# Expert up products of a Mamba and MoE layer: weights stationary, turned rows moving

## The reference, cut to what matters

```python
def _moe(x, gate_w, w1, w2, w3):
    xf = x.reshape(-1, H)
    logits = xf @ gate_w.T
    rw, sel = jax.lax.top_k(logits, TOP_K)
    rw = jax.nn.softmax(rw, axis=-1)
    out = jnp.zeros_like(xf)
    for e in range(E):
        we = jnp.sum(jnp.where(sel == e, rw, 0.0), axis=-1)
        h = jax.nn.silu(xf @ w1[e].T) * (xf @ w3[e].T)      # up products
        out = out + h @ w2[e].T * we[:, None]               # down product
    return out.reshape(B, S, H)
```

## Time and profile before

| | |
|---|---|
| median of 3 runs | 3352.16 us (3351.89 to 3358.85) |
| profiled execution | 3366.11 us |
| its span, first to last instruction | 3364.7 us |
| PE busy over the span | 86% |
| DVE, ACT, POOL busy | 72%, 57%, 32% |
| expert loop | 2844.0 to 3273.5 us |
| steady part of it (2870 to 3262 us) | PE busy 392.00 of 392.00 us |
| gather and sum behind it | 3273.5 to 3364.7 us |

### The profile page before, as it was taken

How to read it: one execution, slowest core, us unless ns; L and a number is a source line. 1 busy time by engine, 2 the same in 40 slices (tenths; PEclk the granted TensorE clock), 3 DMA queues, 4 the chain that set the end, 5 groups by cost and what they waited for, 6 DMA issues and landing times. The chain is left out here.

```text
span 3364.7 us, 45342 instructions
## 1 busy us (share of the span) xinstructions
PE 2891.2 (86%) x12880; PEld 1110.5 (33%) x12881; DVE 2419.1 (72%) x2674; ACT 1913.4 (57%) x3514; POOL 1090.7 (32%) x652
## 2 busy tenths in 40 slices
PE   5798889899765849999999999999999772999990
PEld 1234334334332512222222222222222252666650
DVE  0699999999997758888888888888888173111113
ACT  3556655665642417788787878787887611222220
POOL 2889778778862530000000000000000045000006
PEclk8999999999998969999999999999999975999995
DMA  1111111111111532111111111111110145111114
GB/s 42 42 50 48 41 55 56 38 51 49 40 44 43 180 96 39 39 39 39 39 39 39 39 34 37 37 39 39 39 39 10 43 148 188 44 47 44 46 36 147
DMA packets 123093, 185.25 MB, mean 55 GB/s; under 512 B 30224, under 2 KB 77968, under 8 KB 122896
## 3 DMA queue, kind: packets, MB, share of 16 engines
q1 hardware_dynamic: 109072, 142.95, 15.0%
q0 software_dynamic: 13824, 39.86, 3.7%
HBM read 138.01 MB, written 44.43 MB: 54 GB/s over the span
## 5 line engine op out<-in xcount | busy, mean ns | idle before, releaser
L1529 DVE TENSOR_REDUCE nmh<-ring 128x2 f32<-128x1024 f32 x1024 | 1195.9, 1219 | 198.3 <-PE ring L1406 198.1
L1387 ACT ACTIVATE prob<-s_ps 128x512 f32<-128x512 f32 x2048 | 1073.0, 603 | 284.2 <-PE s_ps L1427 284.2
L767 DVE TENSOR_TENSOR_SCAN h<-dA,state,bx 128x512 f32<-128x512 f32 x512 | 618.0, 1263 | 117.3 <-ACT dA L606 117.3
L391 POOL TENSOR_TENSOR bx<-u,bb 128x2048 f32<-128x2048 f32 x128 | 578.8, 4527 | 193.7 <-DVE h L767 193.5
L1427 PE MATMUL s_ps<-qs,ks 98*128 98x512 bf16 x2048 | 614.8, 388 | 17.9 <-issue 12.2
L1439 PE MATMUL acc<-prob,vst 128*32 128x512 f32 x4096 | 550.0, 609 | 0.2 <-ACT prob L1387 0.2
L606 ACT ACTIVATE dA<-dt,aneg 128x512 f32<-128x512 f32 x512 | 348.8, 691 | 270.4 <-DVE h L767 270.3
L673 PE MATMUL y_ps<-h,ident 128*128 128x512 f32 x1024 | 480.4, 613 | 1.1 <-DVE h L774 1.1
L1406 PE MATMUL ring<-k,q 64*128 64x512 bf16 x2048 | 348.6, 395 | 43.6 <-DMA k<-parts 23.9
L1427 PEld LDWEIGHTS s_ps<-qs,ks 98*128 98x128 bf16 x2048 | 149.4, 97 | 582.4 <-ACT prob L1387 474.9
L774 DVE TENSOR_TENSOR h<-h,c_ps 128x2048 f32<-128x2048 f32 x128 | 289.6, 2262 | 4.5 <-PE c_ps L652 4.2
(11 more groups left out here) (221 smaller groups left out, 2562.9 us busy)
## 6 DMA issues: line engine op xcount, KB each, us to landing
bb<-b_rows SPq DMA_DIRECT2D x128, 256.0 KB, 3.2
q<-parts SPq DMA_DIRECT2D x256, 64.0 KB, 2.1
parts<-part POOLq DMA_DIRECT2D x48, 256.0 KB, 3.1
qs<-parts SPq DMA_DIRECT2D x192, 64.0 KB, 2.7
ks<-parts SPq DMA_DIRECT2D x192, 64.0 KB, 2.8
xt<-slots_in POOLq DMA_DIRECT2D x72, 128.0 KB, 2.3
slots_out<-yt SPq DMA_DIRECT2D x72, 128.0 KB, 1.7
k<-parts SPq DMA_DIRECT2D x256, 32.0 KB, 2.0
```

The source lines that it names most:

```text
L391: nc.gpsimd.tensor_tensor(bx[:, n % BR], u[:, b], bb[:, n % RB, None, :].to_broadcast([P, KI, CH]), ALU.mult).then_inc(s_bx, 1)
L767: nc.vector.tensor_tensor_scan(h[:, n % HR, d, :], dA[:, d % 2, :], bx[:, n % BR, d, :], state[:, b, n, d:d + 1], ALU.mult, ALU.add).then_ ...
L1387: nc.scalar.activation(prob[:, k % PR, j, :], s_ps[:, tile % SR, :], ACT.Exp, scale=SC).then_inc(s_exp, 1)
L1529: nc.vector.tensor_reduce(nmh[:, slot, t, 2 * s:2 * s + 2], ring[:, s, :, :], AX.X, ALU.max, negate=True).then_inc(s_free[s], 1)
```

## The change

The up products change sides. The stationary operand is now a 128x128 piece of the expert's weights, and the moving operand is `xT`, 128 columns (rows of x). The product then has the inner features in the partitions, which is the form the down product needs, so that the four transposes of `mid` and ACT's copy of them go. The 4 matmuls of 512 columns become 16 matmuls of 128 columns.

A piece of weights as stationary operand is read from a fixed place: for each tile DVE copies the expert's `w1` and ACT its `w3` (128 partitions x 1024 floats each) into `wu`, two slots. Both engines read the expert's number into a register for that (`weights_of`). DVE's product now writes `midT` directly. PE's order in a step becomes: rows of j+1 turned, up products of j, down product of j-1. PE reads the expert's number once a tile, just ahead of the down product, not twice. `wu` takes the room of `g`, which moves to the scope of part (2); since that memory is used again in part (3), POOL now waits for its scatters at the end of part (2), ahead of the common wait of all engines, and not only at the start of part (3).

```diff
@@ part (2), end of POOL's program
+                pool.wait_ge(s_sc, 16 * (2 * NT + NE))
...
+            wu = sb3("wu", [P, 2, 2, KM, FI])
-            m_ps = ps3("m_ps", [P, KF, P])
...
+            def weights_of(eng, w, j):
+                e = eng.value_load(expert[0:1, bass.ds(j, 1)], min_val=0, max_val=NE - 1)
+                return w[:, bass.ds(e, 1), :, :].rearrange("p o k n -> p (o k n)")
@@ ACT
+                def gather_w3(j, q):
+                    src = weights_of(act, w3, j)
+                    wait(act, s_up, j - 1)
+                    nc.scalar.copy(wu[:, q % 2, 1].rearrange("p k n -> p (k n)"), src).then_inc(s_wu3, 1)
...
-                    if there(j, 1):
-                        wait(act, s_mp, j)
-                        wait(act, s_dn, j - 2)
-                        nc.scalar.copy(midT[:, (q - 1) % 2], m_ps[:, :, :]).then_inc(s_mT, 1)
+                        gather_w3(j + 1, (q + 1) % 4)
@@ DVE
+                def gather_w1(j, q):
+                    src = weights_of(dve, w1, j)
+                    wait(dve, s_up, j - 1)
+                    nc.vector.tensor_copy(wu[:, q % 2, 0].rearrange("p k n -> p (k n)"), src).then_inc(s_wu1, 1)
...
-                        wait(dve, s_mp, j - 1)
-                        nc.vector.tensor_tensor(mid[:, q % 2, :], sl[:, q % 2, :], c_ps[:, q % 2, :], ALU.mult
+                        wait(dve, s_dn, j - 1)
+                        nc.vector.tensor_tensor(midT[:, q % 2].rearrange("p k n -> p (k n)"), sl[:, q % 2, :],
+                                                c_ps[:, q % 2, :], ALU.mult).then_inc(s_mid, 1)
@@ PE
+                def up(j, q):
+                    wait(pe, s_xT, KM * (j + 1))
+                    wait(pe, s_wu1, j + 1)
+                    wait(pe, s_wu3, j + 1)
+                    wait(pe, s_mid, j - 1)
+                    for w, dst in ((0, a_ps), (1, c_ps)):
+                        for m in range(KF):
+                            for k in range(KM):
+                                last = nc.tensor.matmul(dst[:, q % 2, m * P:(m + 1) * P],
+                                                        wu[:, q % 2, w, k, m * P:(m + 1) * P], xT[:, q % 2, k, :],
+                                                        start=(k == 0), stop=(k == KM - 1))
+                    last.then_inc(s_up, 1)
...
-                    if there(j, 1):
-                        wait(pe, s_mid, j)
-                        wait(pe, s_mT, j - 1)
-                        for m in range(KF):
-                            last = nc.tensor.transpose(m_ps[:, m, :], mid[:, (q - 1) % 2, m * P:(m + 1) * P],
-                                                       ident[:, :])
-                        last.then_inc(s_mp, 1)
-                    if there(j, 0):
-                        wait(pe, s_xT, KM * (j + 1))
-                        wait(pe, s_mid, j - 1)
-                        for w, dst in ((w1, a_ps), (w3, c_ps)):
-                            for k in range(KM):
-                                last = nc.tensor.matmul(dst[:, q % 2, :], xT[:, q % 2, k, :],
-                                                        of_expert(w, e_up, k), start=(k == 0), stop=(k == KM - 1))
-                        last.then_inc(s_up, 1)
+                    if there(j, 0):
+                        up(j, q)
+                    if there(j, 1):
+                        down(j - 1, (q - 1) % 4)
```

More of the change, by code:

```diff
@@ L1610, in moe_stage @@
         ident = sb("m_ident", [P, P])
-        g = sb("g", [P, NT, DM])
         sh = sb("sh", [P, 2, NT])
@@ L1631, in ps2 @@
                 return ctx2.enter_context(nc.psum_tensor(name, shape, dt))
+            g = sb2("g", [P, NT, DM])
             wo = sb2("wo", [P, KM, DM])
@@ L2130, in moe_stage @@
             sl = sb3("sl", [P, 2, FI])
-            mid = sb3("mid", [P, 2, FI])
+            wu = sb3("wu", [P, 2, 2, KM, FI])
             midT = sb3("midT", [P, 2, KF, P])
@@ L2145, in moe_stage @@
             s_mid = sem("m_mid")
-            s_mp = sem("m_mp")
-            s_mT = sem("m_mT")
+            s_wu1 = sem("m_wu1")
+            s_wu3 = sem("m_wu3")
             s_dn = sem("m_dn")
@@ L2161, in every_tile @@
                         step(4 * n + q, q, n)
-                for j in range(NJ - 4, NJ + 2):
+                for j in range(NJ - 4, NJ + 1):
                     step(j, j % 4, j // 4)
@@ L2202, in _, with rows @@
                     sp.wait_ge(s_y[slot], 16 * (NJ // 4))
+            def weights_of(eng, w, j):
+                e = eng.value_load(expert[0:1, bass.ds(j, 1)], min_val=0, max_val=NE - 1)
+                return w[:, bass.ds(e, 1), :, :].rearrange("p o k n -> p (o k n)")
             @block.scalar
             def _(act):
-                def rows(j, q, n):
+                act.wait_ge(s_we, 16 * 3 * NE)
+                def rows(j, q):
                     wait(act, s_xp, j + 1)
@@ L2211, in rows @@
                                              scale=ln2[:, k:k + 1]).then_inc(s_xT, 1)
+                def gather_w3(j, q):
+                    src = weights_of(act, w3, j)
+                    wait(act, s_up, j - 1)
+                    nc.scalar.copy(wu[:, q % 2, 1].rearrange("p k n -> p (k n)"), src).then_inc(s_wu3, 1)
                 def step(j, q, n):
                     if isinstance(j, int) and j == 0:
-                        rows(0, 0, 0)
+                        rows(0, 0)
+                        gather_w3(0, 0)
                     if there(j, -1):
-                        rows(j + 1, (q + 1) % 4, 0)
-                    if there(j, 1):
-                        wait(act, s_mp, j)
-                        wait(act, s_dn, j - 2)
-                        nc.scalar.copy(midT[:, (q - 1) % 2], m_ps[:, :, :]).then_inc(s_mT, 1)
+                        rows(j + 1, (q + 1) % 4)
+                        gather_w3(j + 1, (q + 1) % 4)
                     if there(j, 0):
@@ L2230, in _, with take_y @@
             def _(dve):
+                dve.wait_ge(s_we, 16 * 3 * NE)
+                def gather_w1(j, q):
+                    src = weights_of(dve, w1, j)
+                    wait(dve, s_up, j - 1)
+                    nc.vector.tensor_copy(wu[:, q % 2, 0].rearrange("p k n -> p (k n)"), src).then_inc(s_wu1, 1)
+                def take_y(j, q, n):
+                    slot, taken = at(q, n, 2)
+                    wait(dve, s_dn, j - 1)
+                    wait(dve, s_y[slot], 16 * taken)
+                    nc.vector.tensor_copy(yt[:, slot, :], o_ps[:, q % 2, 0:DM]).then_inc(s_yt, 1)
                 def step(j, q, n):
+                    if isinstance(j, int) and j == 0:
+                        gather_w1(0, 0)
+                    if there(j, -1):
+                        gather_w1(j + 1, (q + 1) % 4)
                     if there(j, 2):
[L2233 to L2236, removed]
+                        take_y(j, q, n)
                     if there(j, 0):
                         wait(dve, s_sl, j + 1)
-                        wait(dve, s_mp, j - 1)
-                        nc.vector.tensor_tensor(mid[:, q % 2, :], sl[:, q % 2, :], c_ps[:, q % 2, :], ALU.mult
-                                                ).then_inc(s_mid, 1)
+                        wait(dve, s_dn, j - 1)
+                        nc.vector.tensor_tensor(midT[:, q % 2].rearrange("p k n -> p (k n)"), sl[:, q % 2, :],
+                                                c_ps[:, q % 2, :], ALU.mult).then_inc(s_mid, 1)
                 every_tile(dve, step)
+                take_y(NJ + 1, (NJ + 1) % 4, (NJ + 1) // 4)
             @block.tensor
@@ L2255, in turn_rows, with down @@
                     last.then_inc(s_xp, 1)
[L2257 to L2261, removed]
+                def up(j, q):
[10 more added lines that the diff above has]
+                    last.then_inc(s_up, 1)
+                def down(j, q):
+                    e = pe.value_load(expert[0:1, bass.ds(j, 1)], min_val=0, max_val=NE - 1)
+                    wait(pe, s_mid, j + 1)
+                    wait(pe, s_yt, j - 1)
+                    for m in range(KF):
+                        last = nc.tensor.matmul(o_ps[:, q % 2, 0:DM], midT[:, q % 2, m, :],
+                                                w2[:, bass.ds(e, 1), m, :].rearrange("p o n -> p (o n)"),
+                                                start=(m == 0), stop=(m == KF - 1))
+                    last.then_inc(s_dn, 1)
                 def step(j, q, n):
```

9 lines of the change are left out of this document (removed).

## The result

The changed kernel takes 3331.02 us (median of 4 runs, 3327.79 to 3338.20) against 3352.93 us before (4 runs): a ratio of 0.9928, 95% interval 0.9904 to 0.9952, 21.9 us less. Forecast were 3328 us, range 3320 to 3353.

The account below looks back on a forecast made before the run. PE was taken to bound the expert loop. Loop -22.7, start -0.3 and end -1.4 us sum to -24.4 us, from the median of 3352.16 to 3327.8 us (3328); range 3320 to 3353.

Parts of the forecast that it names:

- What bounds: Expert loop: PE is busy for all of 392.00 us, so the loop changes only with its instructions' time on PE.
- The pair: Up products: a weight load and its 128-column matmul overlap in full and take the larger time, 0.111 us.
- c: Time of one load and matmul pair of 128 columns in the up products: 0.111 us, between 0.109 and 0.113.
- The first rival: Up products: the load is not hidden by so short a matmul; decides from 0.121 us, up to 3565 us; chance 13%.
- The transposes: Four transposes of `mid` on PE, 0.110 us each, go: 0.44 us a tile.
- The tile and its multiple: Steady loop on PE: 5.50 us a tile against 5.82, 22.7 us less for 71 tiles.
- the sum of the trace: Whole kernel: -22.7 - 0.3 - 1.4 = -24.4 us on the profiled execution of 3366.11 us.
- ACT and DVE: Copies of weights in the loop: some 3.0 us of 5.50 on each engine, at no cost while PE is late.
- The register read: PE, ahead of the down product: 0.7 us of read hidden by ten queued pairs, 1.1 us; cost nothing.
- The edges: Start and end of the expert loop: -0.3 us at the start and -1.4 us at the end.
- The way in: Last scatter to first up product: +0.7 us for POOL's moved wait, some 0.2 us for ACT's first copy.
- The gains: Loop's ends: PE's 1.19 us wait for the first tile's `mid` goes, and the end shortens by 1.4 us.

Follow-up runs that it names:

- The half-sized kernels: The changed kernel with up products of half the moving columns (3328.8 us), half the stationary weight columns (3344.95 us), or both halved (3238.19 us).
- the kernel that was only split: The kernel before with its up products cut into 16 matmuls of 128 moving columns, transposes and ACT's copy kept: 3378.31 us, ratio 1.0041.

## Why the prediction was right

**What bounds.** PE's busy time of 368.00 of 368.00 us and the missing PE waits confirm that the loop is worth what PE's instructions take. One reading was loose: the wait of 0.2 us in the earlier trace rows was the only one for another engine, and the load path stood idle for 133 us besides with no releaser, since it had few loads beside long matmuls; that cost nothing.

**The pair.** Forecast c = 0.111, between 0.109 and 0.113; measured 0.1116. The argument rested on two things: that the gate product's pace, not the 190 ns of the record, is what a load costs, and that it overlaps with a matmul of the same length. The half-sized kernels show both: 0.112 a pair where only the load binds, 0.109 where only the matmul does. The first rival, that the load is not hidden, would have needed 0.121. The value 0.111 itself was in part luck, a middle between two readings of the gate product that each took in an edge of its chain. From its second matmul on, the trace of the kernel before has

```profile
2691.27 1.82 PE L1904 MATMUL g_ps<-gate,gT 128*128 128x8 f32 x15
```

and, up to the transpose behind it, (2692.95 - 2691.27) / 15 = 0.112, the measured price to the last digit; the first matmul took 0.13, and that was in the 0.113. The Trainium skill, TensorE: Matmul & The Clock Gate, section LDWEIGHTS, gives columns divided by 1.2 GHz for a load, 107 ns for 128; the trace is near it but above, with 0.112 us a pair where only the load binds. Its section Back-to-back issue gap gives 81 ns for a pair of 128 columns and 56 for the matmul alone; a price like these 25 ns does not show here: the measured 0.1116 stands 0.003 above the matmul's 0.109.

**The transposes.** Forecast 0.44 a tile, measured 0.44 with them alone taken out.

**The tile and its multiple.** 5.50 forecast, 5.52 measured; 71 x 0.30 = 21.3 us where I had 22.7. The term is c, 0.0006 too small in each of 32 pairs, and its 1.4 us are nearly all that the sum of the trace missed by.

**ACT and DVE.** Hidden as forecast, with the slack even larger: ACT waits 1.9 us for its silu input (I had 1.1), and DVE's copy took 694 ns, not the 1213 of its bound.

**The register read.** Hidden as forecast, by 1.1 us. I took the queue for ten pairs from what it held in the kernel before; it holds 17.

**The edges.** The way in is the term that was mis-sized. I had +0.9 us for it (0.7 and 0.2); it was +2.04. POOL's idle time ahead of its first load grew by 1.2 us and not 0.7 (I had taken DVE's border from the earlier trace rows for POOL's), POOL's first issue by 0.5 beside DVE's copies, which I had not seen at all, and PE waits 0.66 us for ACT's copy where it had stood 0.33 with no releaser. The gains, 1.2 for the first tile's wait and 1.4 at the end, came as forecast, and 0.8 in the first tile on top, whose up products I had left out: in the kernel before they last 6.34 us, from 2848.91 to

```profile
2855.25 0.38 PE L2253 MATMUL x_ps<-m_ident,xt 128*128 128x128 f32 x2
```

and in the changed one 5.55. That this gain nearly makes up for the way in, so that the edges come to -1.4 us where I had -1.7, is luck; the first tile, 5.77 us to the second `a_ps` here, takes 5.53 to 5.79 over the kernels whose first tile is the same. In all -22.9 us in the trace where the sum was -24.4, and -21.9 in the medians.

## What to carry to other kernels

Cost a weight load by its pace in a chain (here 0.112 us for 128 float32 columns), counted clear of the chain's two ends and not by its record, and a pair of load and matmul by the larger of the two: then cutting matmuls down to 128 moving columns costs 4% on them, here 0.14 us a tile, which two transposes of 0.11 us pay for. Short matmuls use up what they otherwise hide: register reads and the turn of the hardware loop, which were free behind matmuls of 0.43 us, showed behind matmuls of 0.11 in the kernel that was only split (0.31 us at each turn of the loop). For a change that touches one stage, compare that stage's stretch between two events; the stages ahead of it, whose code is the same in all kernels here, moved by more than half of the gain from one profiled execution to the next.

## What the runs showed of the hardware that I had not expected

- A stationary operand of 64 columns between ones of 128 costs 0.14 us at the change to 64 and 0.19 at the change back, more than the shorter load gives back where the matmul binds (tile 5.78 against 5.52 us).
- A pair of a float32 load and matmul of 128 columns takes 0.112 us whichever operand is stationary, with or without copies beside it, and whether 128, 64 or 8 columns stream.
- PE's sequencer runs 17 pairs of short matmuls ahead, in two kernels alike; that covers 1.9 us.
- DVE's copy of 1024 floats from SBUF to SBUF took 694 ns where its two-input operation took 1213 and ACT's copy 1045, and POOL's DMA issue beside it 1.06 us, against 0.59 without. The Trainium skill, DMA: Bandwidth & Descriptors, section SWDGE vs HWDGE vs iDMA, says that DVE's mode with two ports locks GpSimd out of the SBUF state that it writes for its descriptors; the trace agrees with 1.06 against 0.59 us, though no run here separates the mode from the copy.
